# Two small roots moved from GpSimd to ScalarE, one dt sum moved later, and the last of 16 states added by ScalarE and TensorE instead of VectorE

## The reference

```python
proj = h @ W_in.T; x, gate = proj[..., :1024], proj[..., 1024:]
x = silu(causal_conv4(x) + conv_b)
ts, B, C = split(x @ W_x.T, [32, 16, 16]); each = each * rsqrt(mean(each**2) + 1e-6)
dt = softplus(ts @ W_dt.T + b_dt); A = -exp(A_log)
def step(state, t):                      # state: 1024 channels x 16
    state = state * exp(dt_t * A) + (dt_t * x_t) * B_t
    y_t = sum over the 16 states of state * C_t
y = (y + x * D) * silu(gate); x1 = x0 + ga * (y @ W_out.T)
h = layernorm(x1) * (1 + cb) + sb; out = x1 + gb * (base(h) + experts(h))
```

## Time and profile before

| what | value |
|---|---|
| time, median of 3 runs | 1514.07 us (1514.06 to 1514.89) |
| the profiled execution | 1512.44 us, span 1510.3 us, mean granted TensorE clock 0.959 |
| VectorE busy | 1213.1 us (80% of the span) |
| TensorE busy | 1349.8 us (89%) |
| GpSimd busy | 1028.2 us (68%) |
| ScalarE busy | 952.1 us (63%) |
| scans of layer 1 on VectorE | 512 instructions, 595.8 us |
| `add_state` on VectorE | 384 instructions, 267.9 us |

### The profile page before, as it was taken

How to read it: one execution, slowest core, us unless ns; L and a number is a source line. 1 busy time by engine, 2 the same in 40 slices (tenths; PEclk the granted TensorE clock), 3 DMA queues, 4 the chain that set the end, 5 groups by cost and what they waited for, 6 DMA issues and landing times.

```text
span 1510.3 us, 25293 instructions
## 1 busy us (share of the span) xinstructions
PE 1349.8 (89%) x8817; PEld 1006.2 (67%) x8817; DVE 1213.1 (80%) x1643; ACT 952.1 (63%) x2617; POOL 1028.2 (68%) x697
## 2 busy tenths in 40 slices
PE   6899999999999959699899899899899999988677
PEld 5566677768776748568668667667766766855543
DVE  5794674556443469999999999999999999999994
ACT  3432343233321577788888897798798888886761
POOL 0353242313212398998998999899899899899870
PEclk9799999999999979899999999999999999999689
DMA  9531222101100200100110110020030020020001
GB/s 331 195 112 37 91 79 84 56 29 36 36 29 15 87 18 1 57 29 15 57 42 1 57 57 1 31 83 1 15 99 1 15 86 14 1 71 29 1 1 42
DMA packets 32388, 77.16 MB, mean 51 GB/s; under 512 B 3667, under 2 KB 4723, under 8 KB 31750
## 3 DMA queue, kind: packets, MB, share of 16 engines
q1 hardware_dynamic: 32262, 75.55, 15.1%
HBM read 66.99 MB, written 8.55 MB: 50 GB/s over the span
## 4 chain that ended last, share of the span: by engine, by line
PE 31%; POOL 13%; DVE 12%; ACT 6%; issue 5%; DVEq 0%; ACTq 0%; POOLq 0%
PE ps_h L1502 10%; DVE h L2273 7%; POOL h L2131 7%; POOL dbu L2097 6%; PE ps_m L1466 4%; DVE acc L2289 3%; ACT ps_a L1757 2%; PE ps_o L1526 2%; PE ps_m L165 2%; PE ps_s L1466 2%; PE ps_m L166 2%; PE ps_m L167 2%; PE ps_m L1426 2%; ACT ab L1889 1%; PE ps_s L165 1%
## 5 line engine op out<-in xcount | busy, mean ns | idle before, releaser
L2273 DVE TENSOR_TENSOR_SCAN h<-ps_a,dbu 128x512 f32<-128x512 f32 x512 | 595.8, 1205 | 21.3 <-ACT ps_a L1757 7.1
L2097 POOL TENSOR_TENSOR dbu<-dtu,b_all 128x1020 f32<-128x1020 f32 x256 | 598.3, 2358 | 14.4 <-DVE h L2273 13.9
L1757 ACT ACTIVATE ps_a<-dt,a_neg 128x256 f32<-128x256 f32 (+1 forms) x1024 | 442.9, 466 | 67.7 <-DVE h L2273 66.6
L1502 PE MATMUL ps_h<-ident,h 128*128 128x128 f32 x1536 | 226.4, 290 | 65.3 <-DVE acc L2289 60.0
L2289 DVE SCALAR_TENSOR_TENSOR acc<-ps_h,c_cur,acc 128x512 f32<-128x512 f32 x384 | 267.9, 737 | 16.9 <-PE ps_h L1502 16.3
L1502 PEld LDWEIGHTS ps_h<-ident,h 128*128 128x128 f32 x1536 | 183.1, 149 | 123.0 <-DVE h L2273 82.4
L724 POOL TENSOR_TENSOR hid_l<-hid,hid_h 128x256 f16<-128x256 f32 (+1 forms) x88 | 77.4, 883 | 155.0 <-ACT hid_h L610 154.8
L2131 POOL TENSOR_TENSOR h<-h,c_all 128x1024 f32<-128x1024 f32 x64 | 151.1, 2362 | 19.2 <-ACT carry L1777 19.2
L602 ACT ACTIVATE sil<-ps_gu 128x256 f32<-128x256 f32 (+1 forms) x88 | 33.9, 385 | 180.6 <-PE ps_gu L167 180.6
L165 PE MATMUL ps_m<-h_h,wi_h 128*128 128x256 f16 x432 | 119.4, 276 | 2.6 <-PEq L155 2.4
L166 PE MATMUL ps_m<-h_l,wi_h 128*128 128x256 f16 x432 | 119.2, 276 | 0.0
(11 more groups left out here) (406 smaller groups left out, 2876.8 us busy)
## 6 DMA issues: line engine op xcount, KB each, us to landing
b_all<-bt_scratch SPq DMA_DIRECT2D x32, 512.0 KB, 3.9
wm<-in_wmod SPq DMA_DIRECT2D x7, 1024.0 KB, 5.2
wo<-in_wmod SPq DMA_DIRECT2D x5, 1024.0 KB, 8.6
xa<-in_x SPq DMA_DIRECT2D x8, 512.0 KB, 4.5
stage<-in_W_in SPq DMA_DIRECT2D x4, 1024.0 KB
x_scratch<-x SPq DMA_DIRECT2D x8, 512.0 KB, 3.1
c_all<-bt_scratch SPq DMA_DIRECT2D x8, 512.0 KB, 6.0
x<-x_scratch SPq DMA_DIRECT2D x8, 512.0 KB, 3.6
```

Source lines behind the costliest of these rows:

```text
L1502: tr = pe.transpose(ps_h[:, t, j * P:(j + 1) * P], h[:, s % RING, j, t * P:(t + 1) * P], W["ident"][:])
L1757: ex = nc.scalar.activation(ps_a[:, j, j % 2:], dt[:, m, j % 2:], ACT.Exp, scale=a_neg[:, m, st:st + 1])
L2097: nc.gpsimd.tensor_tensor(dbu[:, s % AHEAD, :, 1:], dtu[:, :, 1:], b_all[:, st, 1:].unsqueeze(1).to_broadcast([P, DG, CH - 1]), ALU.mult). ...
L2273: nc.vector.tensor_tensor_scan(h[:, s % RING, two].rearrange("p j t -> p (j t)"), ps_a[:, two].rearrange("p j t -> p (j t)"), dbu[:, s % A ...
```

## The change

1. **Roots.** `rms_pow(n)` leaves GpSimd: ScalarE computes exp(-0.5 ln(ms + eps)) in two small instructions (`rms_root`). `inv_std_a(n)` leaves GpSimd for five small ones on ScalarE. The load of the table set that has Ln moves from slot 23 to slot 20.
2. **dt sum.** `dt_add(i, 1)` on GpSimd moves from slot 7 to slot 12, behind `inv_std_b`. `first_decay(i, 1)` moves from slot 8 to 10 and `d_u(i, 1)` from 10 to 12 on ScalarE. `old_state(i, 1)` moves from slot 12 into `first_inputs` at slot 15.
3. **Last state.** State 15 of each group is no longer added on VectorE. ScalarE scales the turned state by C (`weigh_last_state`, two instructions a group, into the tiles `ab` or `h4_h` and `h4_l`), and TensorE adds it in PSUM to the turned `acc` (four more transposes in every `turn_y`). It stands on ScalarE at slot 15 for group 0 and, for group 1, after the decays of step 0 of the next iteration.
4. **Places.** `turn_y(p, 6)` moves from step 1 to 2, `out_projection(p, 2)` likewise, `make_y(p, 4)` from step 1 to 2 and `make_y(p, 6)` from 2 to 3.

```diff
-YB_AT = {0: (4,), 1: (6,)}
+YB_AT = {0: (4,), 2: (6,)}
+MAKE_YB_AT = {2: (4,), 3: (6,)}
-WO_AT = {0: (1,), 1: (2,), 3: (3,), 4: (4,), 6: (5, 6), 7: (7,)}
+WO_AT = {0: (1,), 2: (2,), 3: (3,), 4: (4,), 6: (5, 6), 7: (7,)}
+DT_ADD_AT = 12
...
     # TensorE, turn_y
             if m % DG == 0:
-                pe.wait_ge(S["hT_used"], added_at(i, NS - 1 if m == 0 else STEPS - 1, TT - 1))
+                pe.wait_ge(S["hT_used"], added_at(i, NS - 2 if m == 0 else STEPS - 2, TT - 1))
             for j in range(2):
                 for t in range(TT):
-                    tr = pe.transpose(ps_s[:, j * CH + t * P:j * CH + (t + 1) * P], acc[:, t, (m + j) * P:(m + j + 1) * P], W["ident"][:])
+                    pe.matmul(ps_s[:, j * CH + t * P:j * CH + (t + 1) * P], acc[:, t, (m + j) * P:(m + j + 1) * P], W["ident"][:],
+                              is_transpose=True, start=(j == 0 and t == 0), stop=False, skip_group_check=True)
+            if m % DG == 0:
+                pe.wait_ge(S["last_weighed"], last_weighed_at(i, m // DG, TT - 1))
+            for j in range(2):
+                for t in range(TT):
+                    at = (m % DG + j) * P
+                    tr = pe.matmul(ps_s[:, j * CH + t * P:j * CH + (t + 1) * P], last_of[m // DG][t][:, at:at + P], W["ident"][:],
+                                   is_transpose=True, start=False, stop=True, skip_group_check=True)
...
     # ScalarE
+        def rms_root(n):
+            act.wait_ge(S["ms_done"], n * 2 + 2)
+            nc.scalar.activation(mse[:], msq[:], ACT.Ln, bias=rms_eps[:]).then_inc(S["me_done"], 1)
+            act.wait_ge(S["me_done"], n + 1)
+            nc.scalar.activation(rms[:], mse[:], ACT.Exp, scale=-0.5).then_inc(S["rms_done"], 1)
...
+        def weigh_last_state(i, g):
+
+            act.wait_ge(S["c_done"], i + 1)
+            if g == 0:
+                act.wait_ge(S["init_done"], i * NDG + 1)
+            else:
+                act.wait_ge(S["base_mm"], i * TT)
+                act.wait_ge(S["aggr_a"], TT)
+            for t in range(TT):
+                act.wait_ge(S["hT_done"], turned_at(i, use_of_step((g + 1) * NS - 1), t))
+                nc.scalar.activation(last_of[g][t], ps_h[:, t], ACT.Copy, scale=c_cur[:, t, NS - 1:NS]).then_inc(S["last_weighed"], 1)
...
+            if s == NS - 1:
+                weigh_last_state(i, 0)
-            if s == 8:
+            if s == (8 if first else 10):
                 first_decay(i, 1)
-            if s == 10:
+            if s == (10 if first else 12):
                 d_u(i, 1)
-                if s == 23:
+                if s == WX_AT + 3:
                     nc.scalar.preload_act_table_set("natural_log_exp_and_others")
+                if s == WX_AT + 4:
+                    rms_root(n)
+                if n < LASTC and s == RA_AT + 7:
+                    inv_std_a(n)
...
                 if s:
                     others(i, p, n, first, s - 1)
+                elif not first:
+                    weigh_last_state(i - 1, NDG - 1)
...
     # GpSimd
-            if n is not None and n < LASTC and s == RA_AT + 7:
-                inv_std_a(n)
-            if s == 7:
-                dt_add(i, 1, first)
             if p is not None and s == 12:
                 inv_std_b(p)
+            if s == (7 if first else DT_ADD_AT):
+                dt_add(i, 1, first)
-            if s == 12:
+            if first and s == 12:
                 old_state(i, 1)
-                if n is not None and s == WX_AT + 5:
-                    rms_pow(n)
...
     # VectorE
-                elif (st == 0 or st > JOIN_AT + 2) and not (first and s == 0):
-                    add_state(i if s else i - 1, (s - 1) % STEPS)
+                elif st > JOIN_AT + 2:
+                    add_state(i, s - 1)
                 if p is not None:
-                    for m in at_slot(YB_AT, s):
+                    for m in MAKE_YB_AT.get(s, ()):
                         make_y(p, m)
```

More of the change, by code:

```diff
@@ L1161, in layer_1 @@
     nmr = sb("nmr", [P, TT], F32, c)
+    rms_eps = sb("rms_eps", [P, 1], F32, c)
     rl = sb("rl", [P, TT, RA], F32, c)
@@ L1197, in layer_1, with last_weighed_at @@
     USES = NDG * (NS - KC + 1)
-    ADDS = NDG * (NS - KC)
+    ADDS = NDG * (NS - KC - 1)
     def add_of_step(s):
-        return (s // NS) * (NS - KC) + s % NS - KC
+        return (s // NS) * (NS - KC - 1) + s % NS - KC
     def added_at(i, s, t):
         return (i * ADDS + add_of_step(s)) * TT + (t + 1)
+    def last_weighed_at(i, g, t):
+        return (i * NDG + g) * TT + (t + 1)
+    last_t = (ab[:, 0:DG].rearrange("p k t -> p (k t)")[:, 0:D], ab[:, 0:DG].rearrange("p k t -> p (k t)")[:, D:2 * D])
+    last_of = (last_t, [v[:].rearrange("p k t -> p (k t)").bitcast(F32) for v in (h4_h, h4_l)])
     def joined_at(i, g, t):
@@ L1617, in iteration @@
                     gate_tile(i, 6)
+                if s == 0 and not first:
+                    gate_tile(i, 7)
                 if p is not None:
@@ L1620, in iteration @@
                         turn_y(p, m)
-                if s == 0 and not first:
-                    gate_tile(i, 7)
                 if n is not None:
@@ L1905, in tsb_in, with inv_std_a @@
             nc.scalar.activation(b0[:], ps_s[:, CH:CH + NS], ACT.Copy).then_inc(S["b0_done"], 1)
+        def rms_root(n):
[3 more added lines that the diff above has]
+            nc.scalar.activation(rms[:], mse[:], ACT.Exp, scale=-0.5).then_inc(S["rms_done"], 1)
+        def inv_std_a(n):
+            at = (n + 1) * TT
+            act.wait_ge(S["aggr_a"], n * TT + TT)
+            nc.scalar.activation(veps[:], var_a[:], ACT.Ln, bias=W["epsilon"][:, 0:1]).then_inc(S["inv_a"], 1)
+            act.wait_ge(S["inv_a"], n * 3 + 1)
+            nc.scalar.activation(rstd[:], veps[:], ACT.Exp, scale=-0.5).then_inc(S["inv_a"], 1)
+            act.wait_ge(S["inv_a"], n * 3 + 2)
+            for t in range(TT):
+                op = nc.scalar.activation(nm[:, t:t + 1], nms_a[:, at + t:at + t + 1], ACT.Copy, scale=rstd[:, t:t + 1])
+            op.then_inc(S["inv_a"], 1)
+            act.wait_ge(S["inv_a"], n * 3 + 3)
+            nc.scalar.activation(nmr[:], nm[:], ACT.Copy, scale=ROOT).then_inc(S["nmr_a"], 1)
         def router_in(p):
@@ L1939, in keep_c @@
                 act.wait_ge(S["hT_used"], i * (ADDS * TT))
+                act.wait_ge(S["last_weighed"], i * (NDG * TT))
             act.wait_ge(S["ssn_done"], i * 2 + 2)
             nc.scalar.activation(c_cur[:], ssn[:, :, RDT + NS:], ACT.Copy).then_inc(S["c_done"], 1)
+        def weigh_last_state(i, g):
[5 more added lines that the diff above has]
+                act.wait_ge(S["aggr_a"], TT)
+            for t in range(TT):
+                act.wait_ge(S["hT_done"], turned_at(i, use_of_step((g + 1) * NS - 1), t))
+                nc.scalar.activation(last_of[g][t], ps_h[:, t], ACT.Copy, scale=c_cur[:, t, NS - 1:NS]).then_inc(S["last_weighed"], 1)
         def join_acc(i, g, first):
@@ L1959, in others @@
             if p is not None and s == 9:
+                act.wait_ge(S["y_mm"], value(p, KI // 2, KI // 2 - 1))
                 variance_b(p)
@@ L2011, in others @@
                         dt_abs(n, m)
-                if s == 23:
+                if s == WX_AT + 3:
                     nc.scalar.preload_act_table_set("natural_log_exp_and_others")
-                    if p is not None:
-                        router_exp(p)
-                        router_share(p)
+                if s == WX_AT + 4:
+                    rms_root(n)
+                if n < LASTC and s == RA_AT + 7:
+                    inv_std_a(n)
+                if s == 23 and p is not None:
+                    router_exp(p)
+                    router_share(p)
                 if s == 25:
@@ L2076, in _ @@
         iteration(LASTC, LASTC - 1, None, False)
+        weigh_last_state(LASTC, NDG - 1)
         for t in range(TT):
@@ L2121, in first_inputs @@
             op.then_inc(S["fold_done"], 1)
+            if g and n:
+                old_state(n, g)
             pool.wait_ge(S["fold_done"], (n * 2 + g) * 3 + 2)
@@ L2245, in _ @@
         rms_pow(0)
-        pool.wait_ge(S["begun"], 6)
+        pool.wait_ge(S["begun"], 7)
         first_inputs(0, 0)
@@ L2454, in _ @@
         nc.vector.memset(root[:], ROOT).then_inc(S["begun"], 1)
+        nc.vector.memset(rms_eps[:], RMS_EPS).then_inc(S["begun"], 1)
         diagonals(0)
```

8 lines of the change are left out of this document (4 added, 4 removed).

## The result

The changed kernel takes 1528.04 us (median of 4 runs, 1524.13 to 1529.02) against 1514.48 us for the kernel before on the same chip (4 runs, 1514.06 to 1515.46): a ratio of 1.0094, interval 1.0078 to 1.0109. That is 0.9% slower, 13.6 us; the prediction had +7. The profiled execution took 1524.13 us with a span of 1522.3, against 1512.44 and 1510.3, so the traces have 11.7 us to explain (12.0 by the spans).

A forecast was written before the change was run, and what follows sets the result against it. GpSimd bounds from iteration end to step 7 and scans 16 to 23, VectorE elsewhere. Terms 0.2 + 0.9 = 1.1 us in iterations 1 to 6 (6.6), together 7.4, say +7: 1521 us; case range 1513 to 1528, overall 1503 to 1531.

The forecast's parts named there:

- the 0.9 from step 7 to scan 23: Second term of an iteration: net +0.9 us at scan 23, bounds 0 and 1.4.
- Net at step 7: First term of an iteration: scan 6 1.4 us late, almost all inside VectorE's 1.06 us wait; +0.2, bounds -0.1 and +0.6.
- TensorE becomes the bound in steps 3 to 6: Rival: third `add_h` another 1.4 us later, so the stretch costs 1.6 instead of 0.2; 1531 us, chance 0.09.
- The 0.2 us until the logarithm: Before GpSimd's sum: ScalarE's added work leaves 0.3 us until the logarithm, holding GpSimd by 0.2.
- So the two causes overlap: weigh_h starts 0.9 later, not 1.6: Around scan 16: late dt sum and group 0's weighing on ScalarE together delay GpSimd's second-group weighing by 0.9 us.
- The later dt sum: Steps 7 to 16: ScalarE waits 1.5 us at `first_decay`; +0.7 us at scan 16, bounds 0 and 1.5.
- The removal alone moves neither ... so I take 0: Four VectorE adds fewer an iteration (2.8 us) move neither group's fourth weighed state: gain 0, other bound 1.3 us per group.
- The roots: Between step 22 and 24: the 3.1 us GpSimd loses become a wait for the logarithm; listed sign 1 to 2 us.
- Rms root +0.5 and lost `dbu` wait -0.5: Before scan 23: VectorE's `rms_apply` waits for ScalarE's root, +0.5 us; its wait for `dbu` goes, -0.5.
- The table load: ScalarE, slot 20: 1.28 us, holds scan 22 by 0.1 at most; the skill's drain would add about 1.4 us.
- VectorE is simply the bound: Rival: all 22.3 us of the removed adds come off, 1492 us; chance 0.07.
- The end, taken as equal: At the very end: ScalarE's weighing stands in for VectorE's add, taken as equal in time.

The follow-up runs named there:

- part 1 alone: The kernel before with only the roots moved to ScalarE: 1515.99 us, ratio 1.0027 to the kernel before.
- undoing part 1: The changed kernel with rms root and first deviation back on GpSimd and the table load at slot 23: 1527.25 us, ratio 1.0105 to the kernel before.
- nothing but part 3 and its weighing in a good place: The kernel before with part 3, group 0 weighed behind the keeping of scan 16, router products ahead of the turned pair: 1514.80 us, ratio 1.0006.
- the lighter GpSimd: GpSimd's weighings on half the columns, the rest left unweighed: kernel before so cut 1492.01 us; with part 3 alone added, 1487.32 us.
- x9_dt_only: The kernel before with only part 2, the later dt sum: 1517.33 us, ratio 1.0032 to the kernel before.

## Why the prediction was right or wrong

The direction held, and so did the reason for it: the removed adds turned into waits. The sum was about half of what came, 1.1 us an iteration against 2.08. Two of its terms were mis-sized, and each by an overlap that was smaller than laid out: the 0.2 at step 7, by 0.57, and the 0.9 from step 7 to scan 23, by 0.37 (0.69 - 0.11 - 0.19 + 0.88 = 1.27).

- **Net at step 7, "+0.2, with bounds -0.1 and +0.6": measured +0.77, outside its bounds.** I let almost all of scan 6's delay fall into VectorE's wait of 1.06 us. I had scan 6 at 1.4 us late; in the time of before it starts at 914.51 - 4.22 = 910.29, 1.92 after 908.37. TensorE's chain was laid out in the right order, but it began at 902.73 (906.95 - 4.22) and not at 902.3. The add had started 3.40 us after scan 6 (911.77 - 908.37) and now starts 2.26 after it (916.77 - 914.51), with nothing left to give: 1.92 - 1.14 = 0.78. The chain itself was as long as laid out, 914.51 - 906.95 = 7.56 against 7.5. The rival "TensorE becomes the bound in steps 3 to 6" was the right mechanism with too high a price: 0.5 us later than my layout sufficed, not 1.4.
- **The 0.2 us until the logarithm: measured 0.35** (part 1 alone). It doesn't add to the former: with part 4 in, undoing part 1 changes nothing in this stretch. The later of the two chains sets it.
- **"So the two causes overlap: weigh_h starts 0.9 later, not 1.6": they don't.** Scan 16 is 0.58 later from the dt sum (part 2 alone: 0.63), and the first weighing starts another 0.86 later after it (959.67 - 955.91 = 3.76 against 953.27 - 950.37 = 2.90): 1.44 together. I took ScalarE's idle times in slots 13 and 14 as slack that would bring it back ahead of VectorE. Slot 13 did give: its wait fell from 0.80 to 0.17 us. But the wait in slot 14 is 0.90 in both kernels. Before, then after:

```profile
943.23 0.20 ACT L1823 ACTIVATE xw<-hist 128x3 f32<-128x3 f32 x1 [0.80 <-PE ps_m L167]
...
947.47 0.20 ACT L1823 ACTIVATE xw<-hist 128x3 f32<-128x3 f32 x1 [0.90 <-PE ps_m L167]
...
950.37 2.34 DVE L2273 TENSOR_TENSOR_SCAN h<-ps_a,dbu 128x512 f32<-128x512 f32 x2
```

```profile
948.78 0.20 ACT L1841 ACTIVATE xw<-hist 128x3 f32<-128x3 f32 x1 [0.17 <-PE ps_m L169]
```

It ends with TensorE's product, which was late by the same 0.58 as VectorE, so ScalarE came to the weighing as late as VectorE did. Scan 16 (950.37 before) had been kept 0.29 us after its end (953.00 - 952.71) and is now kept 1.13 after it, so 0.8 to 0.9 of the weighing's 1.26 us stood on the path.
- **The later dt sum, +0.7 at scan 16: close.** 0.69 came in steps 7 to 12 and 0.11 went again in steps 12 to 16, so 0.58 at scan 16, with 1.44 us ahead of `first_decay` where 1.5 were predicted.
- **"The removal alone moves neither ... so I take 0": right in size.** In the kernel with nothing but part 3 and its weighing in a good place, an iteration takes 118.13 us against 118.17. The reason that I gave was only half of it, as the lighter GpSimd showed.
- **The roots.** The prediction turned GpSimd's 3.1 us into a wait, yet listed only 1 to 2 us of it as a sign; it is 3.36. **Rms root +0.5 and lost `dbu` wait -0.5: the net was right.** VectorE waits 0.98 for the root, but steps 18 to 23 take no more time with the roots on ScalarE (17.21) than with them on GpSimd (17.34).
- **The table load: right.** It takes 1.28 us and the next instruction starts 1.29 after it, at its new place too. The drain that the Trainium skill (ScalarE: Activation LUTs, section What ACT_TABLE_LOAD costs) adds to every switch doesn't show here either.
- **The rival "VectorE is simply the bound"** gave 1492. The time was 1528, though VectorE lost 19.3 us of work. The Trainium skill (Perfetto Trace Analysis, section Identifying the Most-Contended Engine) says to relieve the engine with the highest occupancy first; this case's trace doesn't bear out a gain from it.
- **The end, taken as equal:** 1.2 us came off behind the last scan, but x9_dt_only, in which nothing changed there, has 0.9 less too, so that isn't shown to be the change.

With the 0.2 ahead of the first scan these terms make up the 12.0 us between the spans. The medians differ by 13.6, as the profiled execution was the shortest of its four; what the longer ones did isn't in a trace.

## What to carry to other kernels

Where four engines are each busy over 80% of a loop, as here, taking work from the busiest one can be worth no more than the distance to the next chain; find that chain before counting the gain, best by lightening one in an experiment. Idle time of an engine is slack only if what ends it doesn't come late for the same reason as the engine itself. When a small piece is moved in an in-order engine, ask of every engine what now stands behind the wait: when the weighing was moved, most of the wait went from GpSimd to TensorE, and it vanished only when the router was let past it.
